# Attention: the rows of maxima issued by GpSimd's queue between its masks, two in each of four steps, in place of SyncE's queue

## What is computed

```python
q = (x @ Wq.T).reshape(B, S, H, dk).transpose(0, 2, 1, 3)
k = (x @ Wk.T).reshape(B, S, H, dk).transpose(0, 2, 1, 3)
v = (x @ Wv.T).reshape(B, S, H, dk).transpose(0, 2, 1, 3)
scores = jnp.einsum('bhqd,bhkd->bhqk', q, k) / jnp.sqrt(jnp.float32(dk))
scores = jnp.where(causal, scores, jnp.finfo(scores.dtype).min)
probs = jax.nn.softmax(scores, axis=-1)
attn = jnp.einsum('bhqk,bhkd->bhqd', probs, v)
```

## Time and profile before

| | |
|---|---|
| median of three runs | 816.4 us (816.14 to 816.53) |
| profiled execution, its own time | 817.79 us |
| span of the profiled execution | 816.1 us |
| mean granted TensorE clock | 0.974 |
| attention's periods | about 41 to 364 us of the span |
| PE busy | 766.9 us, 94% of the span |
| POOL busy | 245.3 us, 30% of the span |
| rows of maxima | 126 DMAs on SP's queue, 2 on ACT's |

### The profile page before, as it was taken

One profiled execution on the slowest core, in us unless ns is written; L12 is line 12 of the kernel. 1 busy time (PEld: TensorE's weight loads), 2 busy tenths in 40 slices (PEclk: granted clock), 3 DMA queues, 4 the chain that ended last, 5 costly groups with the idle time before them and its releaser, 6 DMA issues.

```text
span 816.1 us, 19285 instructions
## 1 busy us (share of the span) xinstructions
PE 766.9 (94%) x6818; PEld 659.2 (81%) x6818; DVE 614.4 (75%) x1269; ACT 481.5 (59%) x935; POOL 245.3 (30%) x337
## 2 busy tenths in 40 slices
PE   7789999999999999969999989999999989999998
PEld 7667777777777777647989879899999969888887
DVE  5578887777787788836888777689999667777755
ACT  3055555555555555655666657577878846666543
POOL 4047752232222333221000010157776550000000
PEclk9799999999999999977999999999999989999999
DMA  6866657666686655567666651000035144777731
GB/s 163 115 125 95 102 98 115 90 96 92 83 149 97 100 88 90 149 235 243 216 219 239 248 195 70 1 1 2 2 108 187 40 182 179 271 269 261 263 136 52
DMA packets 70983, 111.47 MB, mean 137 GB/s; under 512 B 7062, under 2 KB 27959, under 8 KB 70855
## 3 DMA queue, kind: packets, MB, share of 16 engines
q1 hardware_dynamic: 68848, 108.47, 50.8%
q10 hardware_dynamic: 2048, 1.88, 1.2%
HBM read 41.82 MB, written 42.81 MB: 104 GB/s over the span
## 4 chain that ended last, share of the span: by engine, by line
PE 58%; DMA 11%; DVE 10%; SPq 8%; ACT 6%; issue 6%; ACTq 0%; DVEq 0%; POOL 0%; POOLq 0%
PE bank L417 9%; PE bank L419 7%; PE bank L418 7%; DMA stk<-fx 5%; PE pair_a L938 5%; SPq L607 4%; DVE inter L1972 4%; PE bank L952 3%; PE pair_b L907 3%; DMA fx<-fs 3%; PE bank L1278 3%; PE pair_b L1278 3%; SPq L490 2%; PE pair_a L1243 2%; DMA stack<-mrow 2%
## 5 line engine op out<-in xcount | busy, mean ns | idle before, releaser
L417 PE MATMUL bank<-wd_hi,in_hi 128*128 128x256 f32 x512 | 146.6, 286 | 1.1 <-DVE in_lo L1977 0.9
L419 PE MATMUL bank<-wd_hi,in_lo 128*128 128x256 f32 x512 | 145.7, 285 | 0.0
L418 PE MATMUL bank<-wd_lo,in_hi 128*128 128x256 f32 x512 | 145.4, 284 | 0.0
L1794 DVE TENSOR_REDUCE mx<-pair_b 128x6 f32<-128x768 f32 x124 | 117.9, 951 | 33.9 <-PE pair_b L919 31.9
L683 POOL TENSOR_SCALAR_AFFINE_SELECT prob<-prob 128x512 f32<-128x512 f32 x128 | 81.8, 639 | 202.5 <-ACT prob L1405 202.3
L1570 ACT ACTIVATE in_hi<-inter 128x512 fp32r<-128x512 f32 x128 | 80.7, 630 | 104.8 <-DVE inter L1972 103.5
L1405 ACT ACTIVATE prob<-pair_a 128x768 f32<-128x768 f32 x128 | 103.6, 810 | 64.1 <-PE pair_a L938 62.5
L1977 DVE TENSOR_TENSOR in_lo<-inter,in_hi 128x512 fp32r<-128x512 f32 x128 | 88.4, 690 | 60.8 <-ACT in_hi L1570 59.3
L417 PEld LDWEIGHTS bank<-wd_hi,in_hi 128*128 128x128 f32 x512 | 97.8, 191 | 6.6 <-DVE in_lo L1977 1.7
L418 PEld LDWEIGHTS bank<-wd_lo,in_hi 128*128 128x128 f32 x512 | 97.6, 191 | 4.7
L419 PEld LDWEIGHTS bank<-wd_hi,in_lo 128*128 128x128 f32 x512 | 97.6, 191 | 0.0
(11 more groups left out here) (232 smaller groups left out, 1937.5 us busy)
## 6 DMA issues: line engine op xcount, KB each, us to landing
stk<-fx SPq DMA_DIRECT2D x128, 252.0 KB
stack<-stage SPq DMA_DIRECT2D x184, 128.0 KB, 4.5
fx<-fs SPq DMA_DIRECT2D x32, 512.0 KB, 3.6
fx<-fs SPq DMA_DIRECT2D x32, 256.0 KB, 3.7
fx<-fs SPq DMA_DIRECT2D x16, 504.0 KB
fx<-fs SPq DMA_DIRECT2D x16, 252.0 KB
X<-in_attn_a_x SPq DMA_DIRECT2D x14, 256.0 KB, 5.4
result<-X SPq DMA_DIRECT2D x7, 512.0 KB, 7.9
```

The lines of the kernel that those rows point to most:

```text
L417: pe.matmul(dst, l_hi, r_hi, start=first, stop=False)
L418: pe.matmul(dst, l_hi, r_lo, start=False, stop=False)
L419: return pe.matmul(dst, l_lo, r_hi, start=False, stop=last)
L1794: dve.tensor_reduce(mx[:, h, :, p % PR, :], src[:, :, 0:3 * P].rearrange("p n (t k) -> p n t k", t=3), AX.X, ALU.max).then_inc(a_mx, 1)
```

## The change

The four rows of each entry and half leave SP's queue and go into POOL's, as two pairs. The pair a = 0 of (b, h = 1) is issued behind mask 2 and the pair a = 1 behind mask 3; the pairs of (b + 1, h = 0) stand behind masks 6 and 7. Each pair waits for `a_ml`, as before. The rows get their own semaphores `a_mp[h]`, which `shifted` at p = 0 and p = 4 and `split_max` wait for; entry 0, half 0 keeps `a_md` and its issue by SP and ACT.

```diff
-        a_md = [counted(f"a_md{h}", 64) for h in range(2)]
+        a_md = counted("a_md", 64)
+        a_mp = [sem(f"a_mp{h}") for h in range(2)]
...
+        def max_rows_landed(eng, b, h):
+
+            if b == 0 and h == 0:
+                eng.wait_ge(a_md, upto(a_md, 0, 64))
+            else:
+                eng.wait_ge(a_mp[h], 64 * (b + h))
...
-            def max_rows(b, u, h):
-                sp.wait_ge(a_ml, upto(a_ml, b, h + 1))
-                for a in range(2):
-                    for n in range(2):
-                        max_row(sp, u, h, a, n)
...
-                max_rows(b, u, 1)
...
-                if nxt:
-                    max_rows(b + 1, 1 - u, 0)
...
+            def max_rows(b, u, h, a):
+                pool.wait_ge(a_ml, upto(a_ml, b, h + 1))
+                pool.sem_inc(passed_pool, 1)
+                for n in range(2):
+                    max_row(pool, u, h, a, n, a_mp[h])
...
                 for p in range(NP):
                     mask(b, p)
+                    if p in (2, 3):
+                        max_rows(b, u, 1, p - 2)
+                    if p in (6, 7) and nxt:
+                        max_rows(b + 1, 1 - u, 0, p - 6)
...
                 if p % 4 == 0:
-                    pe.wait_ge(a_md[h], upto(a_md[h], b, 64))
+                    max_rows_landed(pe, b, h)
...
                 dve.wait_ge(a_mT, upto(a_mT, b, h + 1))
-                dve.wait_ge(a_md[h], upto(a_md[h], b - 1, 64))
+                if b:
+                    max_rows_landed(dve, b - 1, h)
```

More of the change, by code:

```diff
@@ L485, in stack_rows, with max_row @@
                 eng.dma_start(to, of).then_inc(a_stk[h], 16)
-        def max_row(eng, u, h, a, n):
+        def max_row(eng, u, h, a, n, landed):
             row = HALF * a + K_S + n
             eng.dma_start(stack[row:row + 1, u, h, :, 0, :].bitcast(F32),
-                          mrow[PR * a:PR * a + PR, h, n, :].bitcast(F32)).then_inc(a_md[h], 16)
+                          mrow[PR * a:PR * a + PR, h, n, :].bitcast(F32)).then_inc(landed, 16)
+        def max_rows_landed(eng, b, h):
[3 more added lines that the diff above has]
+                eng.wait_ge(a_mp[h], 64 * (b + h))
         def out_bank(u, q):
@@ L507, in _ @@
             sp.dma_start(X[:, 2 * TB:4 * TB, :], x_t[:, 2 * TB:4 * TB, :]).then_inc(s_x[2], 16)
-            lead(sp, a_stk + a_md + f_.sp)
+            lead(sp, a_stk + [a_md] + f_.sp)
             def stack_half(b, u, h):
@@ L533, in _ @@
                         for n in range(2):
-                            max_row(sp, 0, 0, 0, n)
+                            max_row(sp, 0, 0, 0, n, a_md)
                     sp.wait_ge(a_qkh, upto(a_qkh, b, h + 1))
@@ L1480, in _ @@
             for n in range(2):
-                max_row(act, 0, 0, 1, n)
+                max_row(act, 0, 0, 1, n, a_md)
             high_weights(4)
```

## The result

The changed kernel takes 943.9 us (median of 4 runs, 940.3 to 946.3) against 816.3 us for the kernel before on the same chip: 1.158 times as long, interval [1.154, 1.163]. The forecast was 928.4 us with a range of 870 to 975.

What follows compares the result with a forecast made beforehand. The prediction took PE, busy 94% of the span, as the bound. Waits for rows 76.7, later masks 18.4, clock 19.5 and SP's queue -2.6 sum to 112.0 us; on 816.4 that gives 928.4 us, range 870 to 975.

Steps and rivals of the forecast that it cites:

- the seams: Where two periods meet, `shifted` 0 waits for rows behind mask 7: 2.82 us each, 15 times.
- the clock: PE's stops in attention: one in two drops the clock to 0.50 for 3.4 us, 15 x 1.3 = 19.5 us.
- the end: End of attention: SP loses row issues, -4.9 us, against 2.3 us for period 15's middle; together -2.6 us.
- the middles: Halfway through a period, `shifted` 4 waits for rows behind mask 3: 2.29 us each, 15 times.
- the later masks: Masks 3 and 7 start later behind the first pair's issues and factor pieces: 18.4 us together.
- X: Time from the end of mask 3 or 7 to the landing of the two rows behind it: 3.2 us.
- The quick landing: Rows issued by POOL land 1.14 us after the issue, no longer queued behind six 128 KB transfers.
- My bound from above: Largest X behind masks 3 and 7: two issues at ACT's pace, 2.07 us, plus slow landing, 2.50 us: 4.57 us.
- POOL's issue: Issue of one row's DMA on POOL, taken to last as long as ACT's median, 1.035 us.
- The quick POOL: Rival: behind masks 3 and 7 POOL issues as SP does, clock holds; X = 2.36 us, 870.1 us; chance 0.20.
- The slow POOL: Rival: behind masks 3 and 7 X = 4.57 us and the clock falls at every stop; 990.4 us; chance 0.15.
- The faster case: Rival: rows land within 0.4 to 0.9 us between mask and `shifted`, row waits go; 796.3 us; chance 0.03.

Runs made afterwards that it cites:

- The fill: Changed kernel with small matmuls nobody reads in PE's stops ahead of `shifted` 0 and 4 (64 and 16 of them): 918.7 us.
- The early order with SP held back in period 14: Changed kernel, each pair one mask earlier, SP in period 14 waiting for landed rows before `load_down` and the feed-forward layer's first write: 888.1 us.
- the guarded kernel: Changed kernel with SP waiting, ahead of the six 128 KB transfers of the second `stack_half`, until the rows for the next period have landed: 901.6 us.

## Why the prediction was right

The sign, the place and the mechanism were right: PE loses at the steps behind masks 3 and 7, waits there for the rows' DMA (100.3 us; 70 to 110 was forecast, though from the 15.2 us that hold the weight load's waits too), and the clock falls. The total is 15.5 us above the forecast because three terms were too small (the seams, the clock, the end) and two too large (the middles, the later masks), and more than half of that cancels. That the total came so near is in part luck.

**X, from the mask's end to the landing, was one number for two cases.** "The quick landing ..., since the rows no longer stand behind six 128 KB transfers in one queue" is the step that failed. Leaving the queue did not free the rows of the six transfers; it put them behind the six in time, where SP's order had put them ahead. In the middle X is about 2.0 us (1.0 us to the issues' end, 1.1 to the landing), at the seam 4.78 us in the median. The seams cost 15 x 4.50 = 67.5 us, not 42.3, and the middles 15 x 1.37 = 20.6 us, not 34.4. My bound from above, 4.57 us, came from a slow landing of before; that it is close is luck, and 14 of the 15 seams lie above it.

**POOL's issue** was taken as ACT's 1.035 us. It is 0.52 us for nearly all 124, quicker than SP's 0.59. The text names this as the size that would be wrong "under 0.7". By it most of the 18.4 us for later masks falls away: a mask and two issues take 0.64 + 1.03 = 1.67 us, which fits into every gap without a piece of the factors, and there masks 6 and 7 stand as far apart as before. With a piece it does not fit: at seven places in periods 0 to 3 POOL starts mask 3 or 7 later behind its exponential than before, by 4.1 us together. The prediction's own figure for a quick issue was 5.7 us. The prediction's estimate of X = 3.0 us from the Trainium skill's figures (DMA: Bandwidth & Descriptors, "Latency and other measured facts" and "Anatomy of one DMA — SWDGE (gpsimd) path") is above what the quiet middle shows, 2.0 us. The second section gives its 2.0 us for set-up and completion together, so the estimate counted part of the cost twice.

**The clock.** The number of falls was right: 22 stretches at 0.50 where there were 8, so 14 more against 15 forecast; inside attention it is 17 against 2. But the reason given for the number, one fall in two stops, was not. All 15 seams have a fall, and of the 16 middles only those of periods 14 and 15 do; at the others PE stopped for 0.9 to 1.7 us and the clock stayed at 1.00. The count is right because half of the stops stand at seams. Their length was wrong. I took 3.4 us for each from the earlier trace rows, though the kernel before has a longer one in attention itself (windows, columns as in the earlier trace rows):

```profile
354.50:361.30 6.80, 5.55 (x43) 3.73 (x36) 1.43 (x3) 5.09 (x10) 1.91 (x3) 0.50 0.68 230
```

The 22 add up to 162 us, 7.4 us each, and the seam shown stays at 0.50 for 7.7 us at least. 162 - 44 = 118 us at 1 - 0.50/0.80 would be 44 us of loss; PE's busy time grew by 38.3, not by 19.5. The fill shows that 25 us of it come back when PE is kept at work.

**The end of attention** was forecast at -2.6 us. Periods 14 and 15 grew by 14.4 us instead, 5.1 of which the terms for their own seam and middle account for. SP did issue the feed-forward layer's transfers without the rows in between, but the rows of periods 14 and 15 now share the engines with them: the last pair landed 5.4 us behind mask 3 of period 15. The early order with SP held back in period 14 shows it for that period: its pairs landed 1.1 us behind their issues' end, where without the guard they took 2.7 to 4.9.

**The rivals.** The quick POOL had its issue right and the clock and the seam wrong. The slow POOL had the seam's X nearly right, and its 39 us for the clock are close to the 38.3 measured, but from 30 falls of 3.4 us where there are 14 more of 7.4; the middles it had wrong. The faster case needed X under 0.4 to 0.9 us and behind masks 3 and 7 the best in any run is 2.0. Counted over all steps and not by medians, the 126.9 us are, but for rounding: 71.6 in the 15 seams' steps, 21.7 in the middles', 28.7 in steps 0 and 1, and 7.2 in steps 2 and 4, less 2.2 us by which attention began sooner.

## What to carry to other kernels

Before a small urgent transfer is moved to another engine's queue, list what the old queue put behind it: the order in one queue kept the rows ahead of six large transfers, and without it those cost 3 us at every seam. Issue such a transfer at least one whole step ahead of its reader, behind a wait that is already over when the queue comes to it; a wait that is not over holds back all that follows on that engine. And a stop that PE makes is paid for twice when the clock falls behind it, so price the stretch at 0.50 by its whole length.

## What the runs showed of the hardware that was not expected

A 4 KB DMA was not slower from GpSimd than from SyncE: its issue took 0.52 us against 0.59, and PE's wait for it ended 1.1 us after the issue's end where the engines were quiet, against 1.14 us in the quick case of SP's. The number of falls hardly follows the length of the stop at the seams: the guarded kernel, where the seam shown stops for 1.8 us in place of 4.8, has 21 stretches at 0.50 against 22, though shorter ones (115 us in all against 162). And VectorE's `xn` took up to 3.4 us in place of 0.40 while GpSimd worked without a gap, with no wait in the trace that says so.
